# The inputs of the first network normalised a group ahead on GpSimd

## The chip, the cores and the metric

The kernel runs on one core of a Trainium2 chip. A core has five engines with queues of their own: TensorE (PE, matrix products and transposes into PSUM), VectorE (DVE), ScalarE (ACT), GpSimd (POOL) and SyncE (SP, which here only starts transfers). Each works through its own list of instructions in order, and they meet through semaphores. The metric is the device time of one execution in microseconds (us). Less is better.

## The reference

The program is a stack of four layers, each an attention and a feed-forward network on x of 8192 tokens by 128 numbers, every one of them added to x after a layer norm. The change concerns the network of layer 0:

```python
def _L0_ffn_ref(x, w1, b1, w2, b2):
    def rmsnorm(x):
        return x * jax.lax.rsqrt(jnp.mean(x * x, axis=-1, keepdims=True) + EPS)
    def act_quant(x):
        scale = 127.0 / jnp.clip(jnp.max(jnp.abs(x), axis=-1, keepdims=True), 1e-05)
        q = jnp.clip(jnp.round(x * scale), -128.0, 127.0) / scale
        return x + jax.lax.stop_gradient(q - x)
    def bitlinear(x, w, b):
        xq = act_quant(rmsnorm(x))
        wq = weight_quant(w)
        return jnp.einsum('bsd,fd->bsf', xq, wq) + b
    h = bitlinear(x, w1, b1)
    h = jax.nn.gelu(h, approximate=False)
    return bitlinear(h, w2, b2)
...
x = x + _L0_ffn_ref(_layernorm(x, axis=-1), L0_ffn_w1, L0_ffn_b1, L0_ffn_w2, L0_ffn_b2)
```

`weight_quant` rounds the weights to -1, 0 and 1 times their mean size. The first thing that happens to each token is `_layernorm`: its mean is taken off, and the rest is divided by its deviation.

## The kernel before

The whole x stays in SBUF as `k.x`, 64 tiles of 128 tokens by 128 numbers, with the mean and variance of each token in `k.mv` and one over the deviation in `k.rstd`. The network's phase, `phase_l0_ffn`, works on 16 groups (k.NG) of four tiles (TG = 4), that is on 512 columns of the 128 partitions at a time.

At its start VectorE finishes `k.rstd` (L130, L132), then quantises both weight matrices (L707 to L714) and prepares `rms` (L716). POOL meanwhile clears buffers (L668 to L672), and SP loads weights and stores zeros.

A group then goes through these parts, each named as in the code:

- VectorE `quantise_x`: four L734, one per tile, (x - mean) * rstd into `h`; L739 takes the largest size of each token, the small operations L723 to L742 make scales, four L744 and L746 give the rounded `q`.
- TensorE `turn_q` transposes q, ScalarE `copy_qT` copies it (L633, L634), TensorE `up` multiplies (L600, L601), ScalarE `gelu` (L640) writes `h2`, of 2048 columns, and `squares` (L647) sums the squares of it.
- POOL `rms2`: L685 and L687 (a power) on four columns. VectorE `levels_h`: L752 takes the largest size over 2048 columns, L754 copies POOL's result, and L723 to L757 make the factor; ScalarE `scale` (L654) applies it; VectorE `quantise_h` (L763) rounds into `q2`.
- TensorE `turn_q2` and `down`, with ScalarE `copy_q2T` (L661) between them; VectorE `new_x` adds to x (L772) and takes new statistics (L778, L783) after waiting for POOL's copy of the last ones; POOL `add_bias` (L679) adds the second bias to x beforehand, and `copy_mv` (L692) puts the new statistics into `k.mv`.

What sets the order is the helper `pipeline`. It is given, for each engine, a list of parts with a lag; in step n the engine does the parts in the order of the list, each for group n minus its lag. So in step n VectorE does `new_x` of group n-5, `levels_h` of n-3, `quantise_x` of n, `quantise_h` of n-3. The first eight steps are written out, then a loop on the chip runs the steps 8 to 15, four at a time (`unroll`), and the last ones are written out again. The helper `Chain` counts the steps of a part in a semaphore and waits for them, and `settle` adds one to a semaphore that nobody waits for.

Of the kernel before, what the change touches and what calls it, by code (L numbers as in the profile page):

```python
# [66 lines left out]
def settle(eng, k):  # L67


    eng.sem_inc(k.settled, 1)  # L70
# [453 lines left out]
def phase_l0_ffn(nc, k):  # L524
# [3 lines left out]
    with ExitStack() as ctx:  # L528
        def sb(name, shape, dt=F32):
            return ctx.enter_context(nc.sbuf_tensor(f"l0f_{name}", shape, dt))  # L530

        s = sems(nc, ctx, "l0f", "var_ready std_ready rstd_ready weights b1_loaded cleared w_chain w_part w_sum w_ready half_ready rms_var rms_std "
                 "rms_ready h_chain a_chain q_ready qT_psum qT_ready h_psum gelu_ready rms2_arg rms2_mean rms2_ready b_chain rr_ready scaled "
                 "q2_ready q2T_psum q2T_ready y_psum biased xn_ready stats_chain stats_ready mv_copied zeroed zero_stored")
# [7 lines left out]
        rms = sb("rms", [P, k.NT])  # L542
        h = sb("h", [P, TG, D])
        hq = sb("hq", [P, TG, D])
# [34 lines left out]
        def _(pe):  # L579
# [40 lines left out]

            pipeline(pe, k.NG, [(1, turn_q), (4, turn_q2), (1, up), (4, down)], unroll=RING4)

        @block.scalar
        def _(act):
# [38 lines left out]

            pipeline(act, k.NG, [(2, gelu), (1, copy_qT), (4, copy_q2T), (3, scale), (2, squares)], unroll=RING4)

        @block.gpsimd
        def _(pool):
# [4 lines left out]
            pool.memset(half[:, :], -0.5).then_inc(s.half_ready, 1)  # L672
            pool.wait_ge(s.half_ready, 1)

            def add_bias(g, m):
                pool.wait_ge(s.q_ready, g + 1)
                settle(pool, k)
                x = k.x[:, bass.ds(TG * g, TG), :]
                pool.tensor_tensor(x, x, b2[:, :].unsqueeze(1).to_broadcast([P, TG, D]), ALU.add).then_inc(s.biased, 1)  # L679
# [13 lines left out]

            pipeline(pool, k.NG, [(1, add_bias), (2, rms2), (5, copy_mv)], unroll=RING4)

        @block.vector
        def _(dve):
# [31 lines left out]
            def quantise_x(g, m):  # L729
                chain = Chain(dve, s.a_chain, g, 2 * TG + 8)  # L730
                wait(dve, s.q_ready, g)
                for j in range(TG):
                    t = TG * g + j
                    n = chain.did(dve.tensor_scalar(h[:, j, :], k.x[:, bass.ds(t, 1), :], k.mv[:, bass.ds(t, 1), 0], k.rstd[:, bass.ds(t, 1)],  # L734
                                                    ALU.subtract, ALU.mult))
                chain.wait(n)
                wait(dve, s.gelu_ready, TG * (g - 3))
                chain.did(dve.tensor_copy(sx[:, m, R, :], rms[:, bass.ds(TG * g, TG)]))
                chain.wait(chain.did(dve.tensor_reduce(sx[:, m, AMAX, :], h[:, :, :], AX_X, ALU.max, apply_absolute_value=True)))  # L739
                levels(chain, sx[:, m], wsum[:, 2:3])  # L740
                wait(dve, s.qT_psum, g - 1)
                chain.did(dve.tensor_scalar(sx[:, m, BACK, :], sx[:, m, LEVELS, :], wsum[:, 4:5], None, ALU.mult))  # L742
                for j in range(TG):
                    n = chain.did(dve.tensor_scalar(hq[:, j, :], h[:, j, :], sx[:, m, R, j:j + 1], sx[:, m, LEVELS, j:j + 1], ALU.mult, ALU.mult))  # L744
                chain.wait(n)
                dve.tensor_scalar(q[:, m % 2], hq[:, :, :], ROUND, ROUND, ALU.add, ALU.subtract).then_inc(s.q_ready, 1)  # L746
                chain.close()
# [37 lines left out]

            pipeline(dve, k.NG, [(5, new_x), (3, levels_h), (0, quantise_x), (3, quantise_h)], unroll=RING4)

# [2387 lines left out]
```

## Time and profile before

| What | us |
|---|---|
| median of three runs | 2973.34 |
| lowest and highest | 2971.69 and 2976.85 |
| profiled execution | 2975.72 |
| its span, from the first to the last instruction | 2974.2 |
| VectorE busy, of the span | 2189.5 |
| TensorE busy | 2577.0 |
| ScalarE busy | 1413.7 |
| POOL busy | 440.5 |

The profile is of one execution. It has a page of sums for the whole program, and views of the trace: the timeline (instructions of an engine in order of time, equal ones merged), the groups of instructions by line and shape, and the busy time of each engine within a stretch. The program goes through nine phases with a barrier between them, so a phase ends when its last engine is done, and the phases before and behind don't overlap with it. Times of instructions are counted from the span's start.

### The profile page before, as it was taken

How to read it: one execution, taken by the hardware profiler on the slowest of the kernel's cores; microseconds unless marked ns; L12 is line 12 of the kernel's file. 1: busy time of each engine (PE TensorE's matmuls, PEld its weight loads, DVE VectorE, ACT ScalarE, POOL GpSimd, SP SyncE). 2: the span in 40 equal slices, each digit the busy share in tenths (PEclk: the TensorE clock that was granted, in tenths of full speed). 3: DMA queues.
4: the chain of work that ended last, by engine and by line, in shares of the span. 5: the costliest groups of instructions: out<-in, count | busy, mean ns of one | idle time of the engine just before them, and what ended most of it. 6: DMA issues, size and time to landing. Idle time of an engine off the chain costs nothing. (4 is left out here: it accounts for less than half of the span.)

```text
span 2974.2 us, 67297 instructions
## 1 busy us (share of the span) xinstructions
PE 2577.0 (87%) x24798; PEld 1867.2 (63%) x24798; DVE 2189.5 (74%) x5427; ACT 1413.7 (48%) x2523; POOL 440.5 (15%) x542
## 2 busy tenths in 40 slices
PE   5967669995899999999999789896997977999688
PEld 4734346663787887788788456664774744555338
DVE  6889869997577676776776468888881077999774
ACT  3658868885011111111110277774662444777574
POOL 0022210000000000000000000000341163555104
PEclk9988779998899999999999789998998989999799
DMA  3110000001212211211311000000002331000001
GB/s 95 36 65 1 0 20 16 14 14 69 103 58 86 86 58 63 108 57 57 114 57 58 13 16 17 11 8 26 24 30 78 93 89 37 1 0 0 1 0 57
DMA packets 55559, 128.97 MB, mean 43 GB/s; under 512 B 9716, under 2 KB 21460, under 8 KB 54616
## 3 DMA queue, kind: packets, MB, share of 16 engines
q1 hardware_dynamic: 47864, 106.41, 10.4%
q0 software_dynamic: 7520, 20.34, 2.2%
q8 instruction: 97, 1.59, 0.2%
q14 instruction: 78, 0.64, 0.1%
HBM read 109.41 MB, written 17.30 MB: 43 GB/s over the span
## 5 line engine op out<-in xcount | busy, mean ns | idle before, releaser
L1500 PE MATMUL banks<-l1f_feed,l1f_w 128*128 128x512 f32 x512 | 228.5, 597 | 1.4 <-DVE l1f_feed L1769 1.4
L1443 PE MATMUL banks<-l1f_sums,l1f_mixes 128*128 128x256 f32 x768 | 186.6, 379 | 0.0
L1769 DVE TENSOR_TENSOR l1f_feed<-l1f_aoT,l1f_rwb 128x512 f32<-128x512 f32 x256 | 158.8, 682 | 16.2 <-PE banks L1443 10.3
L1500 PEld LDWEIGHTS banks<-l1f_feed,l1f_w 128*128 128x128 f32 x512 | 95.7, 192 | 108.6 <-issue 89.7
L1443 PEld LDWEIGHTS banks<-l1f_sums,l1f_mixes 128*128 128x128 f32 x768 | 145.9, 190 | 19.8
L1443 PE MATMUL banks<-l1f_feed,l1f_mixes 128*128 128x256 f32 x512 | 135.3, 387 | 22.0 <-DVE l1f_feed L1726 22.0
L1735 DVE TENSOR_TENSOR l1f_sums<-l1f_feed 128x512 f32<-128x512 f32 x128 | 88.5, 691 | 87.7 <-PE banks L1443 83.9
L214 POOL COPY x<-xn 128x512 f32 (+1 forms) x16 | 9.8, 610 | 936.4 <-DVE xn L1786 936.4
L1463 PE MATMUL banks<-l1f_w,l1f_feed 128*128 128x128 f32 x1024 | 136.5, 277 | 0.0
L836 POOL TENSOR_TENSOR l3a_kbd<-l_kT,consts 128x1024 f32<-128x1024 f32 x64 | 121.5, 1898 | 64.5 <-PE banks L871 63.8
L1463 PEld LDWEIGHTS banks<-l1f_w,l1f_feed 128*128 128x128 f32 x1024 | 126.0, 194 | 0.0
L1443 PEld LDWEIGHTS banks<-l1f_feed,l1f_mixes 128*128 128x128 f32 x512 | 93.1, 192 | 40.3 <-DVE l1f_feed L1726 26.0
L1602 ACT COPY xb<-banks 128x512 f32<-128x512 f32 x16 | 9.4, 586 | 212.1 <-PE banks L1500 212.1
L1100 DVE TENSOR_REDUCE l2a_top<-banks 128x16 f32<-128x1024 f32 x64 | 78.3, 1223 | 34.4 <-PE banks L1047 33.5
L1720 DVE TENSOR_TENSOR l1f_feed<-l1f_hT,l1f_rwb 128x512 f32<-128x512 f32 x128 | 87.6, 684 | 20.7 <-PE banks L1500 12.6
L1047 PE MATMUL banks<-l2a_kbd,l2a_qT 64*64 64x512 f32 x512 | 71.1, 624 | 35.0 <-DVE l2a_prob L1103 35.0
L1100 DVE TENSOR_REDUCE l1a_top<-banks 128x16 f32<-128x1024 f32 x64 | 77.8, 1216 | 28.9 <-PE banks L1047 28.8
L1158 POOL COPY mean_var<-mvn 128x8 f32 (+1 forms) x32 | 6.1, 191 | 594.1 <-DVE mvn L1142 594.1
L1253 ACT ACTIVATE l1a_kbd<-banks,l1a_bk,consts 128x512 f32<-128x512 f32 x128 | 91.1, 784 | 5.0 <-PE banks L1221 4.9
L2951 DVE TENSOR_TENSOR l2e_y<-banks,l2f_sets 128x512 f32<-128x512 f32 x16 | 11.1, 692 | 110.4 <-PE banks L2918 110.4
L1056 PEld LDWEIGHTS banks<-consts,l2a_prob 128*128 128x128 f32 x512 | 56.0, 143 | 56.4 <-ACT l2a_prob L1088 31.1
L1088 ACT ACTIVATE l2a_prob<-l2a_prob 128x1024 f32<-128x1024 f32 x64 | 68.4, 1069 | 44.9 <-DVE l2a_prob L1103 44.7
(532 smaller groups left out, 7081.0 us busy)
## 6 DMA issues: line engine op xcount, KB each, us to landing
l1f_rwb<-l1f_shares SPq DMA_DIRECT2D x128, 512.0 KB, 6.8
l0a_ctxT<-in_ctxT SPq DMA_DIRECT2D x16, 256.0 KB
l2f_sent<-l0f_zero SPq DMA_DIRECT2D x4, 1024.0 KB, 7.0
l1a_ctxT<-in_ctxT SPq DMA_DIRECT2D x16, 256.0 KB, 2.6
l2c_ctxT<-in_ctxT SPq DMA_DIRECT2D x16, 256.0 KB, 2.6
l2e_rows<-l2f_sent SPq DMA_DIRECT2D x16, 256.0 KB, 2.7
l2f_answers<-l2e_y POOLq DMA_DIRECT2D x16, 256.0 KB, 2.7
l3p_ctxT<-in_ctxT SPq DMA_DIRECT2D x16, 256.0 KB, 2.7
```

Of the source, the lines that this page charges most:

```text
L836: pool.tensor_tensor(kbd[:, par], r.kT[:, bass.ds(P * t, P)].unsqueeze(1).to_broadcast([P, H // 2, P]), k.headmask8.unsqueeze(2).to_broadc ...
L1047: last = pe.matmul(self.score_banks[a][S * b:S * b + S, :], self.qT[rows, u, keys], self.kbd[rows, u, :, keys], start=mask is None, stop=T ...
L1056: last = pe.transpose(self.pT_banks[n // 4][:, P * (n % 4):P * (n % 4) + P], self.prob[:, r % 2, 2 * n:2 * n + 2, :], self.k.ident[:, :])
L1088: act.activation(all_heads, all_heads, ACT.Exp, scale=self.scale).then_inc(s.exp_ready, 1)
L1100: dve.tensor_reduce(self.top[:, :], self.scores, AX_X, ALU.max).then_inc(s.max_ready, 1)
L1253: last = act.activation(core.kbd[:, u, n, :], k_bank, ACT.Identity, bias=bk[:, n:n + 1], scale=k.headmask8[:, n:n + 1])
L1443: return pe.matmul(prods[:, n, :], left, right, start=(p == 0 and first), stop=(p == PAIRS - 1), skip_group_check=True)
L1463: pe.matmul(v_bank[:, D * j:D * j + D], feed[:, at + 1, c:c + P], w[:, 0, e2 if first else e1, :], start=False, stop=(p == PAIRS - 1), ski ...
L1500: pe.matmul(out_bank, w[:, 1, e, :], feed[:, e % NB, :], start=(e == 0), stop=(e == E - 1)).then_inc(s.y_psum, 1)
L1720: dve.tensor_tensor(two(feed[:, at, :]), two(hT[:, m, 0:GT]), halves[:, 0:4:3, :], ALU.mult).then_inc(s.parts_ready, 1)
L1735: dve.tensor_tensor(sums[:, sm, 0:2, :], two(feed[:, at, :]), two(feed[:, at + 1, :])[:, 0:1, :].to_broadcast([P, 2, HT]), ALU.add).then_i ...
L1769: dve.tensor_tensor(feed[:, e % NB, :], aoT[:, m, :], rwb[:, m, e, :], ALU.mult).then_inc(s.ae_ready, 1)
```

## The change

Line numbers of the new file differ; the numbers in the words below are of the file before unless said otherwise. VectorE's four L734 per group are gone. In their place POOL does two operations on the whole group of 512 columns, `norm`: subtract the mean (L681 of the new file), then multiply by rstd (L684 there), each with the four tokens' values repeated along the 128 columns. `h` has two buffers now, used in turn. `norm` is POOL's first part, with lag 0; every other part on every engine has its lag raised by one, so that `quantise_x` of a group comes a step after its `norm`. New semaphores: `h_centred` between POOL's two operations, `h_ready` for VectorE, and `h_read`, which VectorE raises after the last of its four scalings of a group and POOL's `norm` two groups later waits for. `add_bias` waits for `h_ready` instead of `q_ready`. POOL waits for `rstd_ready` once before its steps.

```diff
-        h = sb("h", [P, TG, D])
+        h = sb("h", [P, 2, TG, D])
...
-            pipeline(pe, k.NG, [(1, turn_q), (4, turn_q2), (1, up), (4, down)], unroll=RING4)
+            pipeline(pe, k.NG, [(2, turn_q), (5, turn_q2), (2, up), (5, down)], unroll=RING4)
...
-            pipeline(act, k.NG, [(2, gelu), (1, copy_qT), (4, copy_q2T), (3, scale), (2, squares)], unroll=RING4)
+            pipeline(act, k.NG, [(3, gelu), (2, copy_qT), (5, copy_q2T), (4, scale), (3, squares)], unroll=RING4)
...
+            pool.wait_ge(s.rstd_ready, 1)
+
+            def norm(g, m):
+                wait(pool, s.h_read, g - 1)
+                settle(pool, k)
+                tiles = bass.ds(TG * g, TG)
+                each = lambda ap: ap.unsqueeze(2).to_broadcast([P, TG, D])
+                pool.tensor_tensor(h[:, m % 2], k.x[:, tiles, :], each(k.mv[:, tiles, 0]), ALU.subtract).then_inc(s.h_centred, 1)
+                pool.wait_ge(s.h_centred, g + 1)
+                settle(pool, k)
+                pool.tensor_tensor(h[:, m % 2], h[:, m % 2], each(k.rstd[:, tiles]), ALU.mult).then_inc(s.h_ready, 1)
 
             def add_bias(g, m):
-                pool.wait_ge(s.q_ready, g + 1)
+                pool.wait_ge(s.h_ready, g + 1)
...
-            pipeline(pool, k.NG, [(1, add_bias), (2, rms2), (5, copy_mv)], unroll=RING4)
+            pipeline(pool, k.NG, [(0, norm), (1, add_bias), (3, rms2), (6, copy_mv)], unroll=RING4)
...
             def quantise_x(g, m):
-                chain = Chain(dve, s.a_chain, g, 2 * TG + 8)
+                chain = Chain(dve, s.a_chain, g, TG + 7)
                 wait(dve, s.q_ready, g)
-                for j in range(TG):
-                    t = TG * g + j
-                    n = chain.did(dve.tensor_scalar(h[:, j, :], k.x[:, bass.ds(t, 1), :], k.mv[:, bass.ds(t, 1), 0], k.rstd[:, bass.ds(t, 1)],
-                                                    ALU.subtract, ALU.mult))
-                chain.wait(n)
+                dve.wait_ge(s.h_ready, g + 1)
...
-            pipeline(dve, k.NG, [(5, new_x), (3, levels_h), (0, quantise_x), (3, quantise_h)], unroll=RING4)
+            pipeline(dve, k.NG, [(6, new_x), (4, levels_h), (1, quantise_x), (4, quantise_h)], unroll=RING4)
```

How POOL's list changes at the start of the phase, behind its last memset (`l0f_half` is a constant, `l0f_b` the second bias), before:

```order
L672 MEMSET l0f_half 128x4
L679 ISA
L679 TENSOR_TENSOR x<-x,l0f_b 128x512 x2
L685 TENSOR_SCALAR l0f_sh<-l0f_sh 128x4
L687 TENSOR_TENSOR l0f_sh<-l0f_sh,l0f_half 128x4
```

and after, `l0f_h` being the normalised group:

```order
L672 MEMSET l0f_half 128x4
L681 ISA
L681 TENSOR_TENSOR l0f_h<-x,mean_var 128x512
L684 TENSOR_TENSOR l0f_h<-l0f_h,rstd 128x512
L681 TENSOR_TENSOR l0f_h<-x,mean_var 128x512
L684 TENSOR_TENSOR l0f_h<-l0f_h,rstd 128x512
L690 TENSOR_TENSOR x<-x,l0f_b 128x512
```

Four operations of 512 columns stand ahead of the first `add_bias` (L690 there), and none of the five waits for a result of the phase's groups. In the last written-out step ahead of the loop, the order on POOL is before:

```order
L679 TENSOR_TENSOR x<-x,l0f_b 128x512
L685 TENSOR_SCALAR l0f_sh<-l0f_sh 128x4
L687 TENSOR_TENSOR l0f_sh<-l0f_sh,l0f_half 128x4
L692 COPY mean_var<-mvn 128x8
L89 UNCONDITIONAL_BRANCH
```

and after:

```order
L681 TENSOR_TENSOR l0f_h<-x,mean_var 128x512
L684 TENSOR_TENSOR l0f_h<-l0f_h,rstd 128x512
L690 TENSOR_TENSOR x<-x,l0f_b 128x512
L696 TENSOR_SCALAR l0f_sh<-l0f_sh 128x4
L698 TENSOR_TENSOR l0f_sh<-l0f_sh,l0f_half 128x4
L703 COPY mean_var<-mvn 128x8
L89 UNCONDITIONAL_BRANCH
```

The three operations of 512 columns follow directly on the copy of the step before, where one did. VectorE's list, whose order else stays, loses the rows L734 of before between `levels_h` and `quantise_x`; from the end of `levels_h` it reads after:

```order
L765 TENSOR_TENSOR l0f_sh<-l0f_sh 128x4
L745 COPY l0f_sx<-l0f_rms 128x4
L746 TENSOR_REDUCE l0f_sx<-l0f_h 128x4
L734 TENSOR_TENSOR l0f_sx<-l0f_sx 128x4
L735 TENSOR_SCALAR l0f_sx<-l0f_sx 128x4
```

Here the copy of the scales follows straight on the factor of `levels_h` (L765, which was L757).

## Rows read from the trace of the kernel before

**Rows 1.** The page's first line.

```profile
span 2974.2 us, 67297 instructions
```

**Rows 2.** Busy time by engine in a stretch of the loop: engine, us, (instructions).

```profile
253.20:349.60 96.40, 69.92 (x392) 39.89 (x392) 88.31 (x313) 78.67 (x162) 27.06 (x32) 0.81 0.00 1
```

**Rows 3.** Timeline of VectorE in a loop step: start, us, instruction, [idle before].

```profile
281.27 2.25 DVE L752 TENSOR_REDUCE l0f_sh<-l0f_h 128x4 f32<-128x2048 f32 x1
...
283.44 0.16 DVE L754 COPY l0f_sh<-l0f_sh 128x4 f32<-128x4 f32 x1
...
284.60 0.16 DVE L757 TENSOR_TENSOR l0f_sh<-l0f_sh 128x4 f32<-128x4 f32 x1
...
284.98 1.16 DVE L734 TENSOR_SCALAR l0f_h<-x,mean_var,rstd 128x128 f32 x4 [0.22 <-issue]
...
286.26 0.17 DVE L738 COPY l0f_sx<-l0f_rms 128x4 f32 x1
...
289.63 1.22 DVE L763 TENSOR_SCALAR l0f_q<-l0f_h 128x2048 bf16<-128x2048 f32 x1
```

**Rows 4.** Timeline of ScalarE and of POOL in the same loop step.

```profile
284.80 2.56 ACT L654 ACTIVATE l0f_h<-l0f_h,l0f_sh 128x512 f32<-128x512 f32 x4 [2.01 <-DVE l0f_sh L757]
...
290.00 0.93 POOL L685 TENSOR_SCALAR l0f_sh<-l0f_sh 128x4 f32<-128x4 f32 x1 [8.54 <-ACT l0f_sq L647]
291.01 1.04 POOL L687 TENSOR_TENSOR l0f_sh<-l0f_sh,l0f_half 128x4 f32<-128x4 f32 x1
292.01 0.19 POOL L692 COPY mean_var<-mvn 128x8 f32 x1
292.16 1.26 POOL L679 TENSOR_TENSOR x<-x,l0f_b 128x512 f32 x1
```

**Rows 5.** Timeline of VectorE and POOL in two early steps.

```profile
189.30 2.07 DVE L734 TENSOR_SCALAR l0f_h<-x,mean_var,rstd 128x128 f32<-128x128 f32 x4
...
189.78 1.26 POOL L679 TENSOR_TENSOR x<-x,l0f_b 128x512 f32<-128x512 f32 x1 [11.52 <-DVE l0f_q L746]
...
202.48 1.27 POOL L679 TENSOR_TENSOR x<-x,l0f_b 128x512 f32<-128x512 f32 x1
202.56 1.21 DVE L754 COPY l0f_sh<-l0f_sh 128x4 f32<-128x4 f32 x1
```

**Rows 6.** Groups of POOL's instructions by shape: busy us, mean ns | idle before.

```profile
L836 POOL TENSOR_TENSOR l3a_kbd<-l_kT,consts 128x1024 f32<-128x1024 f32 x64 | 121.5, 1898 | 64.5 <-PE banks L871 63.8
...
L679 POOL TENSOR_TENSOR x<-x,l0f_b 128x512 f32<-128x512 f32 x8 | 10.2, 1272 | 15.5 <-DVE l0f_q L746 15.5
```

**Rows 7.** Timeline at the start of the phase, POOL and VectorE.

```profile
178.12 0.14 POOL L672 MEMSET l0f_half<- 128x4 f32 x1
...
179.69 0.49 DVE L712 TENSOR_SCALAR l0f_w1f<-l0f_w1f,l0f_wsum 128x512 f32<-128x512 f32 x1
...
180.68 0.43 DVE L714 TENSOR_SCALAR l0f_w<-l0f_w1f 128x512 bf16<-128x512 f32 x1
```

**Rows 8.** Timeline of VectorE: the first, second and fourth L757 of the phase.

```profile
204.76 0.16 DVE L757 TENSOR_TENSOR l0f_sh<-l0f_sh 128x4 f32<-128x4 f32 x1
...
214.13 0.16 DVE L757 TENSOR_TENSOR l0f_sh<-l0f_sh 128x4 f32<-128x4 f32 x1
...
237.14 0.16 DVE L757 TENSOR_TENSOR l0f_sh<-l0f_sh 128x4 f32<-128x4 f32 x1
```

**Rows 9.** Timeline of VectorE and POOL in the last steps.

```profile
356.54 0.16 DVE L757 TENSOR_TENSOR l0f_sh<-l0f_sh 128x4 f32<-128x4 f32 x1
...
363.25 0.19 POOL L692 COPY mean_var<-mvn 128x8 f32<-128x8 f32 x1
363.58 0.18 DVE L783 BATCH_NORM_AGGREGATE mvn<-bn 128x2 f32<-128x6 f32 x1 [0.98 <-POOL mean_var L692]
...
367.19 0.16 DVE L757 TENSOR_TENSOR l0f_sh<-l0f_sh 128x4 f32<-128x4 f32 x1
...
377.83 0.16 DVE L757 TENSOR_TENSOR l0f_sh<-l0f_sh 128x4 f32<-128x4 f32 x1
```

More of the change, by code:

```diff
@@ L532, in phase_l0_ffn @@
         s = sems(nc, ctx, "l0f", "var_ready std_ready rstd_ready weights b1_loaded cleared w_chain w_part w_sum w_ready half_ready rms_var rms_std "
-                 "rms_ready h_chain a_chain q_ready qT_psum qT_ready h_psum gelu_ready rms2_arg rms2_mean rms2_ready b_chain rr_ready scaled "
+                 "rms_ready h_centred h_ready h_read a_chain q_ready qT_psum qT_ready h_psum gelu_ready rms2_arg rms2_mean rms2_ready b_chain rr_ready scaled "
                  "q2_ready q2T_psum q2T_ready y_psum biased xn_ready stats_chain stats_ready mv_copied zeroed zero_stored")
@@ L729, in quantise_x @@
             def quantise_x(g, m):
-                chain = Chain(dve, s.a_chain, g, 2 * TG + 8)
+                chain = Chain(dve, s.a_chain, g, TG + 7)
                 wait(dve, s.q_ready, g)
-                for j in range(TG):
-                    t = TG * g + j
-                    n = chain.did(dve.tensor_scalar(h[:, j, :], k.x[:, bass.ds(t, 1), :], k.mv[:, bass.ds(t, 1), 0], k.rstd[:, bass.ds(t, 1)],
-                                                    ALU.subtract, ALU.mult))
-                chain.wait(n)
+                dve.wait_ge(s.h_ready, g + 1)
                 wait(dve, s.gelu_ready, TG * (g - 3))
                 chain.did(dve.tensor_copy(sx[:, m, R, :], rms[:, bass.ds(TG * g, TG)]))
-                chain.wait(chain.did(dve.tensor_reduce(sx[:, m, AMAX, :], h[:, :, :], AX_X, ALU.max, apply_absolute_value=True)))
+                chain.wait(chain.did(dve.tensor_reduce(sx[:, m, AMAX, :], h[:, m % 2], AX_X, ALU.max, apply_absolute_value=True)))
                 levels(chain, sx[:, m], wsum[:, 2:3])
@@ L743, in quantise_x @@
                 for j in range(TG):
-                    n = chain.did(dve.tensor_scalar(hq[:, j, :], h[:, j, :], sx[:, m, R, j:j + 1], sx[:, m, LEVELS, j:j + 1], ALU.mult, ALU.mult))
-                chain.wait(n)
+                    last = dve.tensor_scalar(hq[:, j, :], h[:, m % 2, j, :], sx[:, m, R, j:j + 1], sx[:, m, LEVELS, j:j + 1], ALU.mult, ALU.mult)
+                    n = chain.did(last) if j < TG - 1 else last.then_inc(s.h_read, 1)
+                dve.wait_ge(s.h_read, g + 1)
                 dve.tensor_scalar(q[:, m % 2], hq[:, :, :], ROUND, ROUND, ALU.add, ALU.subtract).then_inc(s.q_ready, 1)
```

## The prediction

> **What bounds the kernel now.** The change touches only the phase of the first network, of which rows stand here from 178.12 to 377.83 us, out of a span of 2974.2 us [rows 1, 7, 9]; every other phase issues what it issued before, so the question is how much later or earlier this phase ends. I read the busy time by stage first. In the loop of steady steps VectorE (DVE) is busy 88.31 of 96.40 us, TensorE (PE) 69.92, ScalarE (ACT) 78.67, and GpSimd (POOL) 27.06 [rows 2]. VectorE's order of time then shows no real hole: from L752 at 281.27 to L763 at 289.63 one instruction follows the other, and before L734 there is a pause of 0.22 us with the note "issue", no wait for another engine [rows 3]. ScalarE sits 2.01 us per step waiting for L757 [rows 4]. VectorE sets the pace there.
>
> I name E the end of L757 (the factor of `levels_h`), which releases ScalarE's `scale`. Six steps of the loop, E to E, are 356.70 - 284.76 = 71.94 us, 11.99 each [rows 3, 9]. Counting from E = 284.76: L734 starts at E+0.22, L738 at E+1.50, L763 at E+4.87 [rows 3].
>
> **What is removed.** 64 L734 instructions leave VectorE. In a loop step that is all between E and L738 but a little register work: 1.50 us becomes 0 to 0.2, so 1.3 to 1.4 us of VectorE's time per group, 16 groups: about 21 us, if VectorE stayed the bound.
>
> **What is late next.** The last steps, which have neither L734 nor L679 in them, show it. E at 356.70 to E at 367.35 is 10.65 us, though VectorE is idle in it: ScalarE's scale and squares, POOL's `rms2` and then `copy_mv` at 363.25, and only then L783 at 363.58, which waited 0.98 us for POOL [rows 9]. So without any new cost a step can't be shorter than 10.65: a first gain of 1.34 per loop step at most, whatever VectorE saves.
>
> **What is added, and where POOL's operations fall.** POOL gets two operations of 512 columns per group. The nearest row is L679, of the same engine, operation and size: 1.27 us each; the other, of 1024 columns, is 1.90 [rows 6]. The new ones read an operand repeated along the inner dimension, which no row has, so the lower bound is the 0.63 us by which the two rows differ (512 columns without a fixed price) and the upper bound the 1.90 of the double size; I take 1.27, the row of the same size. Idle time of POOL hides them as work. But POOL is in order: after a step's squares it does L685, L687, L692 [rows 4], and then, where L679 stood, now subtract, multiply, L679 without a pause. POOL starts L685 at 290.00 = E+5.24. It then lasted 0.93 us because VectorE's L763 was running until 290.85 [rows 3, 4]; in the new order L763 ends by E+4.7, before it, so the short form is to be expected: L687 ended 0.31+1.04 after L685 began, copy at E+6.55, subtract E+6.7 to 7.95, a semaphore's 0.1, multiply 8.05 to 9.3, L679 9.3 to 10.55.
>
> **The wait that this makes.** A VectorE instruction that copies or scales within SBUF doesn't run beside such a POOL operation. L754, of 4 columns, takes 0.16 us in the loop; beside L679 of 202.48 to 203.75 it took 1.21 and ended at 203.77 [rows 3, 5]. Four L734 took 2.07 us where L679 ran, 1.16 where it did not [rows 3, 5]. Before, L679 of the loop (292.16 to 293.42) fell on the statistics and the start of the long reduce L752, due a step after 281.27, at about 293.3 [rows 3, 4]; nothing of VectorE waits there. Now the train of three is three times as long, and L754 wants to start, by the chain of the last steps, at E+9.33 (10.65 less the 1.16 from L754's end at 283.60 to E at 284.76, less its own 0.16). That is just after L679 started at E+9.3. L754 so ends with L679, at E+10.58, and the rest of `levels_h` follows: E' = E+10.58+1.16 = 11.75. The chain E, squares, `rms2`, copy, the three POOL operations, L754, E is then the bound, on POOL, and VectorE's gain is spent waiting. If VectorE slips in between multiply and L679, the next small instruction is caught instead: 11.5 to 11.9. Against 11.99 the loop gains 0.25, not 1.3.
>
> The Trainium skill's page "SBUF — State Buffer", section "Who interferes with whom", says that the port pair is an exclusive lock for a whole instruction, and that also a VectorE instruction with two SBUF inputs contends with a GpSimd one that reads SBUF. No row here has such a pair in SBUF beside a POOL read. By it L723 would wait too; if it doesn't, a step is 11.5 instead of 11.75 and the sum 2 us lower.
>
> **The sum, part by part.**
> (a) Start. POOL no longer waits for q: both operations for groups 0 and 1 and the first L679, five of 1.27 from 178.3, when the last memset ends, to 184.7, run beside the quantising of the weights. There L712 (0.49) to L714 (0.43) are of the stopped kind, and VectorE goes through them one by one before its first group [rows 7]. Three instructions, each caught by a POOL operation: L714 would end not at 181.11 but between 184.2 (VectorE gets every gap) and 185.5 (only the pauses): +3.1 to +4.4. L734 of group 0 (1.16) is saved. Net +2.6 (2.0 to 3.3). The cover that was there is gone: before, POOL was idle in this stretch.
> (b) Groups 1 and 2. Each cost VectorE 5.55 us: 2.07 and a pause for L734, stretched by L679 [rows 5], and 3.37 from L738 to the end of L746, where in the loop L763 starts [rows 3]. Now the end of the scaling in `quantise_x` (h_read) starts the train of 3.9 us, beside which only the short reduce L739 runs: L723 or L724 is held until it ends, and some 2.2 of the 3.37 are still to come. 6.1 us per group, +0.55 each: +1.1.
> (c) The first `levels_h` and the second. E is at 204.92 before [rows 8]. The first meets L687 and the train of group 4: +1.2, so E is 209.8. The second is 9.37 after it before (214.29, no `new_x` in it yet) [rows 8]; now the POOL chain makes it 11.2: +1.8. The next two are together 23.0 before (237.30 less 214.29), 11.4 and 11.6 after. At the fourth E, 237.30 before [rows 8], we are 2.6+1.1+1.2+1.8 = 6.7 us late.
> (d) From there to the last E before: 377.99 - 237.30 = 140.7 [rows 8, 9]. After: `norm(15)` ends in step 15, so eight intervals have the train, 8 x 11.75 = 94.0, and four have not, 4 x 10.65 = 42.6: 136.6. Gain 4.1 (8 x 11.5: 6.1; 8 x 12.0: 2.1).
> (e) PE, ACT and SP: the lags all grow by one, so each engine keeps its order; SP has no moved DMA. The extra step of depth costs nothing, as step 0 is POOL's alone and covered by the weights; (a) has its price.
> Sum: +6.7 - 4.1 = +2.6 us. The profiled execution took 2975.7, which becomes 2978.3. The median of the runs lies 2.4 below it: 2976.
>
> **Rivals.**
> *The port doesn't matter here* (faster). All gaps fall well and the steps run at 10.65: 12 x 10.65 = 127.8, a gain of 12.9, and the start gains L734's 1.16 + 2 x 2.07, the 1.05 of L754 and about 1.1 to 1.4 in each of three steps: 22 to 23 in all, 2951. Against it stand the two stretched rows [rows 5]. A half of it (weights little delayed, steps near 11.2) gives about -9: 2964. Together 0.17.
> *POOL's new operations are dearer than L679* (slower). The chain holds two of them in eleven steps, and the start four and groups 1 and 2 four: some 30 lie on the path. At 1.27 we are at +2.6; +0.2% is +5.9; so from 0.11 us more, 1.38 us each, the kernel is slower; at 1.6 it is +12, 2986. For it: operands repeated along the inner dimension are not in the trace. Against: both rows fit one price per column. Chance 0.2, with another 0.05 for VectorE losing at every boundary in (a) and (b) and the loop at 12.0.
> *The change doesn't do what it says.* If the three operations of POOL stood elsewhere in its list, the argument would fall; the order of the new file's instructions has them directly behind the copy of the statistics, so I give this nothing.
>
> **How the numbers follow.** Forecast (bound moved to POOL and the port): 0.58, with its own range 2972 to 2980; faster rivals 0.17; slower 0.25. About 0.2% (5.9 us) is what a measurement of this kernel can tell from no change, and the forecast's own range lies within it: faster 0.17, same 0.58, slower 0.25. The range for 8 in 10 reaches to half of the first rival and to the second at 1.6 us: 2962 to 2986.
>
> **What would show it.** VectorE's busy time falls little: L734 goes (16 x 1.16 and the stretched two, some 20 us), but the copy of `levels_h` (L762 in the new file) takes about 1.2 us instead of 0.16 in the loop, and ends with a POOL operation. From E to E is 11.5 to 11.9 in the loop, 10.65 in the last four. The weights' scaling ends 3 to 4 us later. The subtract and multiply take 1.27. ScalarE's wait for `levels_h` stays near 2 us a step. I would be wrong if the loop's steps are near 10.7 (port), if the new operations are above 1.4 us, or if L714's counterpart ends before 182.

## The result, and the profile after

| | before | after |
|---|---|---|
| median of 4 runs each, us | 2973.74 (2971.69 to 2976.85) | 2996.88 (2989.68 to 2998.72) |
| ratio after/before, 95% interval | | 1.007 (1.0055 to 1.0085) |
| profiled execution: span, us | 2974.2 | 2994.0 |

The kernel became slower by 23.1 us at the medians. The forecast was 2976, with a range of 2962 to 2986.

The first thing to do with two traces is to cut both by stage. Each row is the time from the first to the last instruction of one function of the kernel, in the profiled execution:

| stage | before | after | difference |
|---|---|---|---|
| first network (changed) | 216.8 | 214.2 | -2.6 |
| attention behind it | 326.3 | 328.4 | +2.1 |
| second network (not changed) | 963.0 | 983.6 | +20.6 |
| the next attention | 387.5 | 387.4 | -0.1 |

The changed stage gained 2.6 us. The second network, of which no line was touched, lost 20.6. The span's 19.8 is the sum of the first three, less 0.3 elsewhere. The 2.1 us of the attention can't be put down to the change: two kernels further down have VectorE lists that are equal to that of before up to this stage, and it took 326.3 us in one (`e9_before_pad45`) and 328.8 in the other (`e5_before_pad120`), so it differs by as much from run to run.

Where in the second network? VectorE's (DVE) waits, for the tile `l1f_feed` at the head of its loop; columns: who waited, for whom, us in total, times, longest. Before:

```profile
DVE l1f_feed L1720 <- PE banks L1500: 12.6, 4, 3.8
```

After (the same instruction is now L1728, the one behind it L1734):

```profile
DVE l1f_feed L1734 <- issue: 16.2, 4, 4.1
DVE l1f_feed L1728 <- PE banks L1508: 10.6, 4, 2.9
```

The timeline of VectorE after, around the place where its loop (two steps in a pass, five passes) jumps back; columns: start, us, instruction, [idle before it]:

```profile
1130.43 3.67 DVE L1777 TENSOR_TENSOR l1f_feed<-l1f_aoT,l1f_rwb 128x512 f32<-128x512 f32 x6
1136.60 0.69 DVE L1728 TENSOR_TENSOR l1f_feed<-l1f_hT,l1f_rwb 128x512 f32<-128x512 f32 x1 [2.51 <-PE banks L1508]
1141.33 0.69 DVE L1734 TENSOR_TENSOR l1f_feed<-l1f_hT,l1f_rwb 128x512 f32<-128x512 f32 x1 [4.03 <-issue]
1142.14 0.69 DVE L1743 TENSOR_TENSOR l1f_sums<-l1f_feed 128x512 f32<-128x512 f32 x1
```

L1728 and L1734 are two multiplications with nothing between them, and yet 4.03 us pass. The note is "issue": the profile shows no engine and no transfer that VectorE waited for. That happens four times, once for each jump back. The line of the loop itself, with its register and branch instructions in the same stretch (last columns: first and last start), shows a second pause:

```profile
L1334 DVEq COMPARE_BRANCH  x1: 73/73/73, 1130.9 to 1130.9; - x1
L1334 DVEq FUSED_REGOPS  x1: 80/80/80, 1136.3 to 1136.3; - x1
```

From the branch to the first instruction of the next pass VectorE's sequencer needed 5.4 us. Six multiplications were queued and ran meanwhile, so only 2.51 us are seen as idle, and that wait is put down to TensorE (L1508). It wasn't TensorE that ended it: in `e1_after_pad7` below, where the jump is short, the same multiplication starts with no idle before it. The kernel before had this jump too, 6.7 us here:

```profile
L1326 DVEq COMPARE_BRANCH  x1: 67/67/67, 1131.7 to 1131.7; - x1
L1326 DVEq FUSED_REGOPS  x1: 80/80/80, 1138.4 to 1138.4; - x1
```

but not the 4.03 us behind it: L1726 followed L1720 after 0.61.

```profile
1138.68 0.69 DVE L1720 TENSOR_TENSOR l1f_feed<-l1f_hT,l1f_rwb 128x512 f32<-128x512 f32 x1 [3.75 <-PE banks L1500]
1139.29 0.69 DVE L1726 TENSOR_TENSOR l1f_feed<-l1f_hT,l1f_rwb 128x512 f32<-128x512 f32 x1
```

The distance from one new x of this network to the next is 56.5 us where no jump lies between; across a jump it was 58.4, 57.2, 57.4 and 58.3 us before, and 63.0, 63.0, 63.0 and 63.3 after: 21.0 us more in four jumps. That is the whole loss of the stage.

Now the changed stage. A loop step of VectorE and of POOL after, to be held against [rows 3, 4]:

```profile
279.03 1.22 DVE L771 TENSOR_SCALAR l0f_q<-l0f_h 128x2048 bf16<-128x2048 f32 x1
...
282.71 2.25 DVE L760 TENSOR_REDUCE l0f_sh<-l0f_h 128x4 f32<-128x2048 f32 x1
284.88 0.94 DVE L762 COPY l0f_sh<-l0f_sh 128x4 f32<-128x4 f32 x1
...
286.81 0.16 DVE L765 TENSOR_TENSOR l0f_sh<-l0f_sh 128x4 f32<-128x4 f32 x1
```

```profile
280.78 0.23 POOL L696 TENSOR_SCALAR l0f_sh<-l0f_sh 128x4 f32<-128x4 f32 x1 [6.41 <-ACT l0f_sq L647]
281.09 1.04 POOL L698 TENSOR_TENSOR l0f_sh<-l0f_sh,l0f_half 128x4 f32<-128x4 f32 x1
282.09 0.19 POOL L703 COPY mean_var<-mvn 128x8 f32 x1
282.24 1.04 POOL L681 TENSOR_TENSOR l0f_h<-x,mean_var 128x512 f32 x1
283.54 1.04 POOL L684 TENSOR_TENSOR l0f_h<-l0f_h,rstd 128x512 f32<-128x512 f32 x1 [0.26 <-POOL l0f_h L681]
284.53 1.27 POOL L690 TENSOR_TENSOR x<-x,l0f_b 128x512 f32 x1
```

This is the forecast picture: three POOL operations in a row, the copy of four columns (L762) that takes 0.94 us instead of 0.16 and ends, at 285.82, with the third of them, at 285.80. With E the end of L765, the fourth, the twelfth and the last of the stage:

```profile
241.10 0.16 DVE L765 TENSOR_TENSOR l0f_sh<-l0f_sh 128x4 f32<-128x4 f32 x1
...
332.50 0.16 DVE L765 TENSOR_TENSOR l0f_sh<-l0f_sh 128x4 f32<-128x4 f32 x1
...
375.10 0.16 DVE L765 TENSOR_TENSOR l0f_sh<-l0f_sh 128x4 f32<-128x4 f32 x1
```

Eight steps in (332.50 - 241.10) = 91.40, 11.43 each, then four in 42.60, 10.65 each.

### The profile page after: what moved, and what is told of

Its sections match the earlier page's. It is cut to its first block and busy times, and to the rows that moved or that the text cites. A ratio compares the mean times of both kernels' runs of the same rounds, so it can differ in the third digit from the quotient of the medians.

```text
span 2994.0 us, 67245 instructions
## 1 busy us (share of the span) xinstructions
PE 2583.1 (86%) x24798; PEld 1870.3 (62%) x24798; DVE 2187.4 (73%) x5363; ACT 1412.4 (47%) x2523; POOL 466.8 (16%) x574
## 3 DMA queue, kind: packets, MB, share of 16 engines
q8 instruction: 97, 1.59, 0.2%
## 5 line engine op out<-in xcount | busy, mean ns | idle before, releaser
L1508 PE MATMUL banks<-l1f_feed,l1f_w 128*128 128x512 f32 x512 | 228.3, 596 | 1.4 <-DVE l1f_feed L1777 1.4
L1508 PEld LDWEIGHTS banks<-l1f_feed,l1f_w 128*128 128x128 f32 x512 | 95.6, 192 | 108.5 <-issue 89.5
L214 POOL COPY x<-xn 128x512 f32 (+1 forms) x16 | 9.8, 610 | 957.0 <-DVE xn L1794 957.0
L1728 DVE TENSOR_TENSOR l1f_feed<-l1f_hT,l1f_rwb 128x512 f32<-128x512 f32 x128 | 87.8, 686 | 18.6 <-PE banks L1508 10.6
L1734 DVE TENSOR_TENSOR l1f_feed<-l1f_hT,l1f_rwb 128x512 f32<-128x512 f32 x128 | 87.8, 686 | 16.2 <-issue 16.2
```

Of the source, the lines that this page charges most:

```text
L1508: pe.matmul(out_bank, w[:, 1, e, :], feed[:, e % NB, :], start=(e == 0), stop=(e == E - 1)).then_inc(s.y_psum, 1)
L1728: dve.tensor_tensor(two(feed[:, at, :]), two(hT[:, m, 0:GT]), halves[:, 0:4:3, :], ALU.mult).then_inc(s.parts_ready, 1)
L1734: dve.tensor_tensor(two(feed[:, at + 1, :]), two(hT[:, m, HT:GT + HT]), halves[:, 1:3, :], ALU.mult)\
```

## The experiments

The lists of instructions of the built kernels give one more number. VectorE's loop of the second network is 334 instructions long. It starts at place 1946 of VectorE's list before, and at place 1863 after, since the change took 83 instructions net out of the list ahead of it (L734 with its waits and registers, in the written-out steps and in the loop).

### Same work, the loop moved by a few instructions

`e1_after_pad7` is the kernel after, with eight semaphore increments that nothing waits for, in VectorE's list of the second network, ahead of its loop (7 instructions net):

```diff
             dve.wait_ge(s.sigmoid, 1)
+            for _ in range(8):
+                settle(dve, k)
```

> The changed kernel with eight semaphore increments more in VectorE's list (seven once built, since one joins another instruction), at a place in the phase of the second network where VectorE waits 6 us for TensorE, ahead of that phase's loop. Nothing else is changed. Theory A: the 20 us come from where that loop lies in VectorE's instruction memory: in the changed kernel VectorE stands still 4.0 us behind the loop's first multiplication, once per pass, because the next piece of instructions is fetched there. Seven instructions later that piece would begin ahead of the loop: the pause of 4.0 us per pass goes, the phase falls from 983.6 to about 963 us, the whole to 2976 us. Theory B: the work that the change gives POOL and the two buffers lengthen the later phase in another way: 2997 us as before.

Measured: 2963.16 us (2961.43 to 2967.35), beside 2974.26 for before on the same chip: ratio 0.9964 (0.995 to 0.9978). The second network took 955.7 us instead of 983.6, and the steps over the jump 56.5 like the others. The two multiplications (L1730 and L1736 here) at the head of a pass:

```profile
1129.53 0.69 DVE L1730 TENSOR_TENSOR l1f_feed<-l1f_hT,l1f_rwb 128x512 f32<-128x512 f32 x1
1130.13 0.69 DVE L1736 TENSOR_TENSOR l1f_feed<-l1f_hT,l1f_rwb 128x512 f32<-128x512 f32 x1
```

Seven instructions that do nothing took 33.7 us off the median of after. Theory A had the cause and not the size: it counted the pause of 4.0 us alone and expected 963 and 2976 us, but the long jump went as well (5.4 us in after, 0.3 here). In the profiled executions 27.9 of 32.4 us are the second network's; another 2.4 are the next attention's (385.0 instead of 387.4), which took 384.8 and 387.2 in two kernels below with nothing changed in it, so these aren't shown to be the seven instructions' work.

`e2_before_pad173` and `e3_before_pad59` are the kernel before, with 173 and 59 instructions put in at the same place.

> The kernel before with 173 semaphore increments more in VectorE's list at the same idle place, so that the second network's loop starts 256 instructions behind where it starts in the changed kernel; the first network is untouched. Theory A, if the pieces are of 256 instructions: the same pause of 4 us per pass appears in it, and the phase lasts about 20 us longer than 963: 2994 us, and up to 4 more, since 173 increments of 0.05 us outlast the 6.2 us wait that they stand in. Theory B: 2974 to 2978 us, the increments alone.

> The kernel before with 59 such increments at that place. The loop moves by 59 instructions, but by theory A it still lies within two pieces of 256: no new pause, the increments lie in the 6.2 us wait, 2974 us, within 3. If any shift of the loop costs 20 us, about 2994. Theory B: 2974.

Measured: 3006.14 us (ratio 1.0103, 1.0087 to 1.012) and 2968.75 us (0.9983, 0.9974 to 0.9993). With 173 the loop starts at 2119, and before's multiplications show the pause of the kernel after, at the same instruction:

```profile
1149.73 0.69 DVE L1722 TENSOR_TENSOR l1f_feed<-l1f_hT,l1f_rwb 128x512 f32<-128x512 f32 x1 [2.62 <-PE banks L1500]
1154.45 0.69 DVE L1728 TENSOR_TENSOR l1f_feed<-l1f_hT,l1f_rwb 128x512 f32<-128x512 f32 x1 [4.04 <-issue]
```

So a kernel without any part of the change has the loss. (Its time is above that of after, and above the 2994 to 2998 expected, because the increments themselves cost 10.5 us: the first new x of the network came 195.0 us after the stage's start, and 184.5 before. In the trace they follow one another every 0.09 us, not 0.05, so 173 last 16 us, and VectorE's 6.2 us wait there hides only a part.) With 59 even the long jump that before had is gone, which theory A had not foreseen: the total is 2 us under the expected 2971 to 2977. The theory that the loss comes with POOL's new work, or from what it leaves behind, has fallen.

`e4_after_pad83` gives back to after the 83 instructions that it had lost, at the end of VectorE's list of the first network, so that everything behind stands where it stood before.

> The changed kernel with 83 increments at the end of VectorE's list for the first network, so that VectorE's list from the next phase on lies exactly where it lies in the kernel before. Theory A: everything behind the first network takes what it took before; the first network took 214.2 us instead of 216.8 and gets up to 4 us of increments at its end, where VectorE waits 0.6 us: 2971 to 2976 us. Theory B: 2997 us or more.

Measured: 2977.41 us (1.0009, 1.0 to 1.0019); second network 960.1 us, steps over the jump 57.3 to 57.5. With the old place the loss is gone, though all of POOL's new work is still there. The increments themselves cost the first network 7.4 us (221.6, and 214.2 without them), where up to 4 were expected; the total is 1.4 us above the expected 2971 to 2976. The first attention took 330.6 us, 1.8 more than in any other kernel here; why stays open.

### What is it about the place?

Starts 1863 and 2119 were bad (pause at the head and long jump), 1946 middling (long jump alone), 1870 and 2005 good (neither). `e5_before_pad120` puts the start at 2066.

> The kernel before with 121 one-step semaphore increments (120 instructions net) put into VectorE's list ahead of the second network's loop. By the theory of position the loop of 334 instructions now starts near the 200th place of a block of 256 and so lies in three blocks again, as in the kernel after, but with some 60 instructions of it in the first block instead of about four. If what costs is that a pass reaches the end of its first block before the next one has been read, 60 instructions (about 10 us of work) hide the reading: no pause at the head of a pass, steps near 56.5 to 57.5 us, second network 960 to 968 us, total 2965 to 2975 us. If any loop in three blocks pays one reading in each pass, wherever the boundary lies: a pause of about 4 us somewhere in each pass, steps of 58 to 63 us, second network about 980 us, total 2985 to 2996 us. If only the number of instructions ahead counted and not the position: between the 59 and the 173 tried, so a total on a line between 2969 and 3006, about 2989.

Measured: 2982.0 us (1.0028, 1.0016 to 1.0041). No pause at the head, 5.5 to 6.3 us over the jump, steps of 57.2 to 58.1, like before. The second network took 966.8 us, as the first theory expected (960 to 968), but the total lies 7 us above that theory's range, and in none of the others. The expectation had left out what the increments cost: the first new x came 189.0 us after the stage's start and not 184.5. So the pause at the head needs a short head, as the first theory said; but 1946 and 2066 being middling and 2005, between them, being good fits no blocks of 256. (If two blocks of 256 were kept and one began just behind 1863, a loop at 2005 would end nearer to the end of its pair than one at 1946; so 1946 would have to be good too.) It does fit blocks of 128: counted from 1863, the starts seen are 0 and 2x128 + 0 (bad), 7 and 128 + 14 (good), 83 and 128 + 75 (middling). The page's own table of queues bears it out. After:

```profile
q8 instruction: 97, 1.59, 0.2%
q14 instruction: 78, 0.63, 0.1%
```

`e1_after_pad7`:

```profile
q8 instruction: 97, 1.59, 0.2%
q14 instruction: 57, 0.47, 0.1%
```

These are the queues that bring instructions: packets and MB. A packet of q14 has 0.47 MB / 57 = 8.2 KB. The lists of VectorE, ScalarE, GpSimd and SyncE together are 4438 + 1810 + 813 + 354 = 7415 instructions. That is 0.47 MB / 7415 = 63 bytes each, and 7415 / 57 = 130 for a packet; 128 of 64 bytes is an estimate from these and from the spacing of the starts. (A packet of q8 is twice as large, 1.59 MB / 97; TensorE is the engine left for it.) With the loop badly placed 21 more packets are read, about five for each of the four jumps. All good kernels have 57 to 59 here, all others, before among them, 78 or 79.

Two kernels tell 128 from 256, with 45 and 95 instructions put into before:

> The kernel before with 46 increments (45 instructions net) ahead of the second network's VectorE loop, whose 334 instructions then start at place 1991 of VectorE's list. The starts seen so far are 1863 and 2119 (a pause of 4.0 us at the head of each pass and 5.4 to 5.8 us over the jump back), 1870 and 2005 (no pause, 0.3 us over the jump back), 1946 and 2066 (5.4 to 6.7 us over the jump back, no pause at the head). Theory of blocks of 128 instructions, of which the memory keeps three for a loop: 1991 is 1863 + 128, so the loop begins four or five instructions ahead of a block's end and reaches into a fourth block: both pauses, passes of 119.5 us, second network about 984 to 997 us, total 2988 to 3005 us. Theory of blocks of 256, two kept (the Trainium skill, page Runtime: NRT & Kernel Launch, section on instruction fetch, has blocks of 16 KiB, 256 instructions): the loop starts 124 into a block and ends 458 into the pair, which fits: no pause, second network 955 to 957 us, total 2964 to 2970 us.

Measured: 2997.82 us (1.0083, 1.0064 to 1.0102), second network 984.0, steps over the jump 62.8 to 63.8:

```profile
1136.20 0.69 DVE L1722 TENSOR_TENSOR l1f_feed<-l1f_hT,l1f_rwb 128x512 f32<-128x512 f32 x1 [2.55 <-PE banks L1500]
1140.90 0.69 DVE L1728 TENSOR_TENSOR l1f_feed<-l1f_hT,l1f_rwb 128x512 f32<-128x512 f32 x1 [4.01 <-issue]
```

> The kernel before with 96 increments (95 net): the loop of 334 starts at place 2041, 45 instructions behind a boundary by the theory of blocks of 128, and ends 379 behind it, just inside three blocks (384). Theory of three blocks of 128: no pause, 0.3 us over the jump back, passes of 113.0 us, second network 955 to 957 us, total 2964 to 2970 us. If only one or two places (near 1870 and 2005, each 7 to 14 behind a boundary) are good, because the block behind the loop's end is read ahead once a pass comes near it: 5.4 to 6.7 us over the jump back as in the kernel before, second network 961 to 967 us, total 2971 to 2982 us.

Measured: 2972.61 us (0.9996, 0.9986 to 1.0005), 59 packets in q14, all steps 56.5, and the jump (same columns as above) takes 0.3 us:

```profile
L1326 DVEq COMPARE_BRANCH  x1: 67/67/67, 1137.1 to 1137.1; - x1
L1326 DVEq FUSED_REGOPS  x1: 80/80/80, 1137.4 to 1137.4; - x1
```

Both came as blocks of 128 say, in the steps and over the jump. The second's stage (960.3 us) and total missed their ranges, the total by 2.6: the 95 increments cost some 3.5 us at the start of the stage (188.0 instead of 184.5 to the first new x), which the expectation left out. The reading that fits all eight starts is that three blocks of 128 can stay while a loop runs. A loop of 334 is held whole if it starts 2 to 45 places behind a boundary (it ended 379 places behind one at most, of 384) and isn't from some 70 on (404 and more); between the two lies untried ground. If it isn't held, each jump reads again, 5.4 to 6.7 us of which 0.7 to 1.9 reach the step where that is all. If the loop also begins four or five instructions ahead of a boundary, VectorE stands another 4.0 us in front of the second multiplication, which is the loop's fifth instruction, and the step is 6.3 to 8.2 us longer in all; that the next block isn't there yet is the likely reason, and the place of the pause fits it.

The record's other loops agree. In the traces of before and after every other VectorE loop takes 0.2 to 0.4 us over its jump, the longest of them with 293 instructions (the first network's, before), which by this reading starts 70 behind a boundary and ends 363 behind it, within three blocks. By the same reading a loop of at most 257 instructions fits wherever it starts (127 + 257 = 384); in these programs only the loops of 334 and 293 are longer.

The Trainium skill, page "Runtime: NRT & Kernel Launch", section "Instruction fetch mechanics", says that a taken branch whose target isn't in the two pages held forces a read before execution goes on. The traces agree as to the mechanism: 0.3 us over a jump within what is kept, 5.4 to 6.7 over one out of it. The same section gives pages of 16 KiB, 256 instructions; for VectorE the measurements decide, and they fit 128.

### What sets the step of the first network now

These three stand on `e1_after_pad7`, so that the second network is quiet, and 2963.16 us and 213.7 us for the first network are what they are held against. They ran on another chip, though, on which before took 2972.77 us and not 2974.26. So the totals are compared by their ratio to before, 0.9964 (0.995 to 0.9978) for `e1_after_pad7`, which overlaps with the interval of each of the three; the readings rest on the stage and its steps. `e6_bias_one_column` leaves 127 of 128 columns of the second bias out, on POOL:

```diff
-                x = k.x[:, bass.ds(TG * g, TG), :]
-                pool.tensor_tensor(x, x, b2[:, :].unsqueeze(1).to_broadcast([P, TG, D]), ALU.add).then_inc(s.biased, 1)
+                x = k.x[:, bass.ds(TG * g, TG), 0:1]
+                pool.tensor_tensor(x, x, b2[:, 0:1].unsqueeze(1).to_broadcast([P, TG, 1]), ALU.add).then_inc(s.biased, 1)
```

> The kernel after with the 8 increments of the first experiment, and GpSimd adds the second bias to one column of 128 only (the other 127 columns are left out), so its third operation in a row shrinks from 1.27 us to about 0.1. Theory (VectorE's two-buffer operations are stopped while GpSimd works): the copy of four columns in the hidden layer's levels (L762) falls from 0.94 us to its own 0.16 us, the loop step of the first network from 11.43 to 10.65 to 10.75 us, and the first network by 8 x 0.7 to 8 x 0.78 plus up to 1.5 us in the written-out steps: 5.6 to 7.7 us, total 2955.5 to 2958 us beside 2963.2 of the same kernel with the whole bias. Rival (the copy waits for something else, such as GpSimd's power operation or a semaphore): it stays at 0.94 us, the step at 11.43, total 2963.

Measured: 2960.17 us (0.9958, 0.9941 to 0.9975), first network 209.2 us. VectorE's timeline and POOL's:

```profile
281.92 0.16 DVE L762 COPY l0f_sh<-l0f_sh 128x4 f32<-128x4 f32 x1
```

```profile
281.57 0.20 POOL L690 TENSOR_TENSOR x<-x,l0f_b 128x4 f32 x1
```

In the loop the copy is back at 0.16 and most steps at 10.65 to 10.9, though two were 11.6 and one 12.8, so the stage gained 4.5 us where 5.6 to 7.7 were expected, and the total lies 2.2 us above its range. The longer steps were not explained. In the loop the copy had waited for the bias and for nothing else; the first two copies of the stage, which meet the subtract, still took 1.0.

`e7_bias_after_levels` does the whole bias, but at another time:

```diff
             def add_bias(g, m):
                 pool.wait_ge(s.h_ready, g + 1)
+                wait(pool, s.q2_ready, g - 2)
...
-            pipeline(pool, k.NG, [(0, norm), (1, add_bias), (3, rms2), (6, copy_mv)], unroll=RING4)
+            pipeline(pool, k.NG, [(0, norm), (6, copy_mv), (1, add_bias), (3, rms2)], unroll=RING4)
```

> The kernel after with the 8 increments; GpSimd's list in a step becomes normalise, copy mean and variance, add the bias, powers, and the bias waits for the end of VectorE's last rounding (L771), so that it runs beside the new x and its statistics, which read PSUM or one buffer. Theory: the bias then ends 1.3 us after the rounding, the powers and the normalising follow 0.6 to 0.7 us later than now and end at or just behind the maximum (L760); the copy L762 waits 0 to 0.4 us instead of 0.8. Step 10.7 to 11.1 us, total 2957.5 to 2961 us. Rival (new x and its statistics are stopped by GpSimd too): they stretch by about 1 us, step 11.4 or more, total 2963 or more.

Measured: 2958.03 us (2955.87 to 2961.74), ratio 0.9953 (0.9936 to 0.9969); first network 208.1 us, steps of the loop 10.9 to 11.3. The total and most steps came as expected. This is faster than before and than after; that its total beats `e1_after_pad7` is not shown, though its stage is 5.6 us shorter. VectorE's and POOL's timeline:

```profile
276.03 1.12 DVE L781 SCALAR_TENSOR_TENSOR x<-banks,l0f_sh,x 128x128 f32 x4
277.30 0.87 DVE L787 BATCH_NORM_STATS2 bn<-x 128x6 f32 x4 [0.15 <-DVE x L781]
...
280.68 0.54 DVE L763 COPY l0f_sh<-l0f_sh 128x4 f32<-128x4 f32 x1
```

```profile
276.30 1.27 POOL L691 TENSOR_TENSOR x<-x,l0f_b 128x512 f32 x1 [5.93 <-issue]
277.53 0.23 POOL L697 TENSOR_SCALAR l0f_sh<-l0f_sh 128x4 f32<-128x4 f32 x1
...
280.16 1.04 POOL L684 TENSOR_TENSOR l0f_h<-l0f_h,rstd 128x512 f32<-128x512 f32 x1 [0.26 <-POOL l0f_h L681]
```

The new x (L781), which has one input in PSUM, runs beside the bias with its 1.12 us unchanged, and so do the statistics, with one input. (Only their first 0.27 us lie beside the bias; in `e8_bias_in_quantise` they ran beside a whole L681, in 0.87 us too.) What waits is again the copy, here 0.38 us, until POOL's multiply (L684) ends at 281.20.

`e8_bias_in_quantise` starts the bias with the four multiplications by levels, and does the powers first in a step, for a group one step later:

```diff
-                pool.wait_ge(s.h_ready, g + 1)
+                pool.wait_ge(s.a_chain, (TG + 7) * g + 8)
...
-            pipeline(pool, k.NG, [(0, norm), (1, add_bias), (3, rms2), (6, copy_mv)], unroll=RING4)
+            pipeline(pool, k.NG, [(4, rms2), (0, norm), (6, copy_mv), (1, add_bias)], unroll=RING4)
```

> The kernel after with the 8 increments; GpSimd's list in a step becomes powers, normalise, copy mean and variance, add the bias, and the bias waits for VectorE's factor for the way back (L749), so that it starts with the four multiplications by levels (L751, 1.11 us together). Theory: GpSimd is free when VectorE reaches L762 (0.16 us), and the 1.27 us of the bias outlast L751 by about 0.2, which falls on the rounding L754. Step 10.8 to 10.95 us, total 2957.5 to 2960 us. Rival (the multiplications, with both ends in SBUF, are stopped as well): they wait for the whole bias, step 11.7 to 12, total 2965 to 2968.

Measured: 2963.53 us (0.9975, 0.9963 to 0.9986), first network 216.3 us, steps 11.6 to 11.7. The rival had the mechanism right, if a little too dear (2965 to 2968), as VectorE's timeline and POOL's show:

```profile
279.32 2.16 DVE L751 TENSOR_SCALAR l0f_hq<-l0f_h,l0f_sx 128x128 f32<-128x128 f32 x4
```

```profile
279.61 1.27 POOL L690 TENSOR_TENSOR x<-x,l0f_b 128x512 f32 x1 [4.48 <-DVE l0f_sx L749]
```

L751, 1.11 us when alone, took 2.16: each of its four has both ends in SBUF, and they are stopped like the small copy. With L762 free at 0.16 the step is still 0.2 longer than in `e1_after_pad7`.

## Why the prediction was wrong

**The step that failed** is in the first paragraph: "every other phase issues what it issued before, so the question is how much later or earlier this phase ends". The other phases do issue the same instructions. But they stand 83 places earlier in VectorE's list, and a loop's time depends on where it stands: +20.6 us of the span's +19.8. The profile of before had a sign of it, which the prediction didn't use: 78 packets in q14 where about 58 would bring each list once ((4514 + 1810 + 754 + 354) / 128), and four waits of VectorE at a loop's head, 12.6 us, put down to TensorE. None of the rivals was this one either.

**The bound and the wait** were right. The bound of the loop moved to the chain through POOL, and VectorE's saving is spent in front of L762, which `e6_bias_one_column` shows by taking the bias away. ScalarE's wait for `levels_h` came to 1.7 us a step, near the 2 of the forecast.

**POOL's new operations** were taken at 1.27 us each, between 0.63 and 1.90. L681 took 1.03 us at best and L684 1.04, after a pause of 0.26 for the semaphore between them in the loop, where 0.1 was taken. Two of them with their pause are 2.3 us, not 2.6; hence the step of **11.43** instead of 11.75 (11.5 to 11.9), and 10.65 in the last four, as said. From the fourth E to the last it was 375.26 - 241.26 = 134.0 us, a gain of 6.7 where 4.1 was forecast.

**(a) The start** was mis-sized: +0.45 us (the first copy of `quantise_x` at 186.27, and at 185.82 before), not +2.6. The timeline there:

```profile
178.70 1.03 POOL L681 TENSOR_TENSOR l0f_h<-x,mean_var 128x512 f32<-128x512 f32 x1 [0.55 <-POOL l0f_half L672]
...
179.91 1.04 POOL L684 TENSOR_TENSOR l0f_h<-l0f_h,rstd 128x512 f32<-128x512 f32 x1 [0.18 <-POOL l0f_h L681]
180.09 1.15 DVE L724 TENSOR_SCALAR l0f_w1f<-l0f_w1f 128x512 f32<-128x512 f32 x1
...
181.27 1.15 DVE L725 TENSOR_SCALAR l0f_w<-l0f_w1f 128x512 bf16<-128x512 f32 x1
```

L723 (before's L712, [rows 7]) slipped in front of POOL's multiply; the next two waited for one POOL operation each, +0.7 apiece, so the first matrix was ready at 182.42, 1.3 later than 181.11 and not 3.1 to 4.4: two catches where three were counted, and cheaper operations. The second matrix added 0.3, and the 1.16 of L734 came off.

**(b) and (c)**, groups 1 and 2 and the first two E: at the second E the kernel was 218.61 - 214.29 = 4.3 us late and at the fourth 241.26 - 237.30 = 4.0, where 6.7 was forecast. Of the difference 2.1 is (a)'s; (b) and (c) were forecast at 4.1 and came to 3.5. That they came so near is in part luck, for the parts were off both ways: groups 1 and 2 cost 0.4 and not 1.1; the first E 2.3 and not 1.2, since POOL's three operations in a row caught three small instructions one after another (L762, L735 and L736, which took 1.03, 0.98 and 1.19 us) and not one; the second 1.2 and not 1.8; and the next two steps gained 0.4. Here the trace answers what no row of before could:

```profile
191.28 0.59 DVE L734 TENSOR_TENSOR l0f_sx<-l0f_sx 128x4 f32<-128x4 f32 x1
191.90 1.20 DVE L735 TENSOR_SCALAR l0f_sx<-l0f_sx 128x4 f32<-128x4 f32 x1
```

The L734 of after (before's L723) takes 0.16 us elsewhere, and it has two inputs, both in SBUF; it waited too, until POOL's L684 (190.81 to 191.85) ended. That a VectorE instruction with two SBUF inputs contends with a GpSimd one that reads SBUF is what the Trainium skill's page "SBUF — State Buffer", section "Who interferes with whom", says, and the trace agrees. The prediction had left it open between 11.5 and 11.75.

**The sum for the stage** was +2.6 and came to -2.6, from three terms: the start (2.1 too much), the loop's steps (2.6) and (b) with (c) (0.6). Held against a kernel in which the second network is equally quiet, the change itself is worth 217.2 - 213.7 = 3.5 us of the first network (`e3_before_pad59` and `e1_after_pad7`), and 5.6 at the medians of the totals. These two have a spread of their own: over six traces the unchanged stage took 216.7 to 218.5 us, and the changed one 214.2 and 213.7 in two, so it gained 2.5 to 4.8. The other 2.1 us of the medians aren't shown to be the change's: the second network, for one, took 955.7 us in `e1_after_pad7` and 957.0 in `e7_bias_after_levels`, with the same list on VectorE.

**The chances.** "Slower" had 0.25, for dearer POOL operations or lost boundaries; it was slower for neither reason.

## What to carry to other kernels

Adding or removing instructions shifts every later loop of that engine in its instruction list, and a long loop (here one of 334 instructions; those up to 293 were never hit) can change its time by it. Before costing such a change, look at the queues that bring instructions for packets beyond what the lists need, and at waits of one engine that come once per pass at a loop's head. After the change, if a stage that was not touched has moved, put a few empty instructions ahead of its loop and measure again before judging the change. And work that is moved to GpSimd should be laid beside VectorE instructions that read PSUM or that reduce one input. Copies and scalings within SBUF stood still until GpSimd's operation ended, from 4 to 512 columns, and so did an operation with two inputs in SBUF.

## What the runs showed of the hardware

- VectorE's list comes in blocks of 128 instructions (8.2 KB packets), of which a loop may fill three: that is what fits eight starts of one loop. A jump back inside them takes 0.3 us, one out of them 5.4 to 6.7, and a loop of 334 instructions ran 21.0 us slower than before when it stood 83 places earlier, and 5.3 faster when it stood 76 earlier (sums of the four steps with a jump).
- An operand repeated along the inner dimension doesn't slow POOL: L681 and L684 took 1.04 us for 512 columns, L690, where the bias is repeated over the four groups of columns, 1.27.
- A `settle` increment isn't free on VectorE: they follow one another every 0.09 us. The 83 of `e4_after_pad83` cost 7.4 us, and the 173 of `e2_before_pad173` 10.5, since they began in a wait of 6.2.
